# One attention-and-FFN block on one core: where the first FFN's residual x is saved, where its bias is added, and which engine widens and rounds

## What is computed

```
x = x + tanh(g_xattn[0]) * _L0_xattn_ref(ctx, ctx, _layernorm(x), ssm_kernel, D, 8)
x = x + tanh(g_ffn[0]) * _L0_ffn_ref(_layernorm(x), w1, b1, w2, b2)
x = x + tanh(g_xattn[1]) * _L1_xattn_ref(_layernorm(x), ctx, ...)
x = x + tanh(g_ffn[1]) * _L1_ffn_ref(_layernorm(x), ...)
```

```
def _dyn_quant_linear(x, w, b):
    qx, sx = _quant_per_tensor(x)      # one scale for all of x
    qw, sw = _quant_per_channel(w)     # one scale per output row of w
    acc = jnp.matmul(qx.astype(jnp.int32), qw.T.astype(jnp.int32))
    return acc.astype(jnp.float32) * (sx * sw) + b
h = _dyn_quant_linear(hidden_state, w1, b1)      # 512 -> 2048
h = jax.nn.gelu(h, approximate=False)
return _dyn_quant_linear(h, w2, b2)              # 2048 -> 512
```

## Time and profile before

| what | value |
|---|---|
| median of 3 runs | 641.4 us |
| the profiled execution, its own time | 643.1 us |
| its span (first to last instruction) | 641.3 us |
| PE, DVE, ACT, POOL busy | 95%, 85%, 74%, 55% |
| mean granted clock of PE | 0.997 |
| the 64 steps of `mm1` end, `mm2` starts | 283.4 us, 287.5 us |
| `mm2` ends on PE | 343.4 us |

### The profile page before, as it was taken

The page is one execution under the profiler, slowest core; times in us unless marked ns, Lnnn a source line. Parts: engine busy times, 40 slices in busy tenths (PEclk is TensorE's granted clock), DMA queues, the critical chain, the costliest instruction groups (busy, mean ns, idle before and its releaser), DMA issues.

```text
span 641.3 us, 9316 instructions
## 1 busy us (share of the span) xinstructions
PE 609.0 (95%) x2769; PEld 358.2 (56%) x2798; DVE 546.6 (85%) x1066; ACT 473.8 (74%) x718; POOL 351.9 (55%) x430
## 2 busy tenths in 40 slices
PE   5899999999999998989999999999888999999997
PEld 5777777777776443444445556555433444444443
DVE  2697888889999789976779988889898999999964
ACT  4469785765655896888672477766689999999984
POOL 1579888888874292310001111114487989898861
PEclk9999999999999999899999999999999999999999
DMA  8959896799999389838549920000116666656651
GB/s 300 377 192 310 291 327 223 260 323 339 332 299 331 134 285 311 223 94 327 198 98 167 255 56 16 16 17 17 50 33 162 185 177 183 164 180 164 182 162 50
DMA packets 141973, 125.20 MB, mean 195 GB/s; under 512 B 96032, under 2 KB 103984, under 8 KB 140784
## 3 DMA queue, kind: packets, MB, share of 16 engines
q1 hardware_dynamic: 134496, 110.52, 56.8%
q10 hardware_dynamic: 7440, 14.24, 6.6%
HBM read 68.04 MB, written 33.64 MB: 159 GB/s over the span
## 4 chain that ended last, share of the span: by engine, by line
PE 65%; DVE 12%; ACT 7%; issue 6%; DMA 4%; POOL 3%; SPq 2%; ACTq 0%; POOLq 0%; DVEq 0%
PE ps L1195 22%; PE ps L1475 14%; PE ps L1491 8%; PE ps L1313 4%; PE ps L1402 3%; PE ps L1432 3%; PE ps L1344 3%; DMA arena<-in_x 2%; ACT turn L989 2%; POOL arena L663 2%; PE ps L1450 2%; PE ps L1406 2%; SPq L446 2%; PE ps L1204 2%; DMA x_d<-arena 1%
## 5 line engine op out<-in xcount | busy, mean ns | idle before, releaser
L1195 PE MATMUL ps<-arena 128*128 128x288 f32 x640 | 160.6, 407 | 1.6 <-DVE inv_s L1661 0.9
L1195 PEld LDWEIGHTS ps<-arena 128*128 128x128 f32 x640 | 119.4, 190 | 33.5 <-DVE inv_s L1661 0.9
L1475 PE MATMUL ps<-arena 128*128 128x512 bf16 x510 | 113.5, 379 | 4.5 <-DVE arena L2066 4.3
L1475 PEld LDWEIGHTS ps<-arena 128*128 128x128 bf16 x512 | 49.4, 98 | 66.9 <-DVE arena L2066 5.7
L721 POOL TENSOR_TENSOR arena<-arena 128x512 f32<-128x512 f32 x64 | 80.4, 1276 | 8.6 <-DVE arena L2066 7.7
L618 POOL TENSOR_TENSOR arena<-arena 128x1024 f32<-128x1024 f32 x32 | 60.6, 1894 | 19.9 <-issue 12.3
L1313 PE MATMUL ps<-arena 128*128 128x512 bf16 (+1 forms) x249 | 57.1, 387 | 3.7 <-ACT arena L952 3.2
L1491 PE MATMUL ps<-arena 128*128 128x512 bf16 x241 | 57.1, 379 | 1.9 <-ACT arena L1103 0.7
L1344 PE MATMUL ps<-arena 128*128 128x512 bf16 x251 | 55.3, 379 | 1.2 <-DVE arena L1815 0.9
L952 ACT ACTIVATE arena<-ps,b,s 128x512 f32<-128x512 f32 x64 | 48.5, 778 | 10.6 <-DMA x_d<-arena 5.3
L625 POOL TENSOR_TENSOR turn<-turn 128x512 f32<-128x512 f32 x31 | 40.5, 1307 | 20.8 <-DVE turn L1638 20.8
(11 more groups left out here) (231 smaller groups left out, 1274.0 us busy)
## 6 DMA issues: line engine op xcount, KB each, us to landing
arena<-in_L_ffn_w SPq DMA_DIRECT2D x48, 512.0 KB, 6.2
arena<-kpad_d ACTq DMA_DIRECT2D x16, 512.0 KB, 7.1
hq_d<-arena SPq DMA_DIRECT2D x14, 512.0 KB, 2.6
tern_d<-late SPq DMA_DIRECT2D x24, 256.0 KB, 6.2
arena<-in_ctx SPq DMA_DIRECT2D x4, 1024.0 KB, 12.1
arena<-in_x SPq DMA_DIRECT2D x4, 1024.0 KB, 14.8
arena<-in_L_ffn_w ACTq DMA_DIRECT2D x8, 512.0 KB, 5.7
arena<-in_ctx SPq DMA_DIRECT2D x2, 2048.0 KB, 10.3
```

The source lines that it names most:

```text
L1195: last = pe.matmul(ps[:, 4 * s + lo, 0:NB * PAIRS], toep[:, u, (LB - 1 - lo + li) * P:(LB - lo + li) * P], kv[:, s, li, :], start=(li == 0 ...
L1475: last = pe.matmul(ps[:, bank, :], xq4T[:, s, 4 * j + k, :], w[:, k, c * L:(c + 1) * L], start=(k == 0), stop=(k == LB - 1))
```

## The change

1. SP saves x1 without its bias, as soon as each group of four tiles is complete: `x1_save(0)` and `(1)` follow the second `ctx_early` load, `(2)` and `(3)` the load of W2's block 0. They wait for the tiles (`x1_made`), no longer for POOL.
2. POOL adds the bias to `x_res` after it has come back, tile by tile in the order of use, after `partition_all_reduce`: 16 additions of 128 x 512 float32. DVE's `to_residual(k)` waits for `xb_added` of its tile in the place of `rows_in`.
3. `turned_widen(2)` and `(3)` move from DVE to POOL.
4. W2's blocks 2 and 3 are rounded by ACT, after 4 and after 12 gelus of the third group; DVE keeps blocks 0 and 1.
5. On SP, `w2_store(0)` moves ahead of the two transposing loads of x1.

```diff
+            def x1_save(g):
+                for n in range(G * g, G * g + G):
+                    x1_made(sp, n)
+                t = order1[G * g]
+                rows = slice(t, t + TB * (G - 1) + 1, TB)
+                sp.dma_start(x1_d[:, rows, :], x_res[:, rows, :]).then_inc(S["x1_saved"], 16)
+
+            x1_save(0)
+            x1_save(1)
             for c in range(4):
                 sp.wait_ge(tint_out[c], 16 * TC // 4)
             sp.dma_start(raw2[0], w2c[0]).then_inc(w2_in[0], 16)
+            x1_save(2)
+            x1_save(3)
...
-            x1_save(0)
             x1q_store(2)
             x1q_store(3)
-            x1_save(1)
+            w2_store(0)
             x1q_turned(2)
-            x1_save(2)
             x1q_turned(3)
-            w2_store(0)
-            x1_save(3)
             w2_store(1)
...
-            pool.wait_ge(S["b2_ready"], 1)
-            pool.wait_ge(S["xn1_ready"], NT)
-            pool.wait_ge(S["xqb_ready"], 3)
-            for t in order1[:10]:
-                pool.tensor_tensor(x_res[:, t, :], x_res[:, t, :], b2b[:, :], ALU.add).then_inc(S["xb_added"], 1)
-            pool.wait_ge(S["xqi_ready"], NG)
-            for t in order1[10:]:
-                pool.tensor_tensor(x_res[:, t, :], x_res[:, t, :], b2b[:, :], ALU.add).then_inc(S["xb_added"], 1)
+            def turned_widen(g):
+                rows = xqT[:, :, g * L:(g + 1) * L]
+                pool.wait_ge(w1_raw[g - 2], 16 * W1_LOADS + 16)
+                pool.tensor_scalar(rows, rows.bitcast(I16), 1.0, 0.0, ALU.mult, ALU.add).then_inc(S["xq_out"], 1)
+
+            turned_widen(2)
+            turned_widen(3)
...
+            pool.wait_ge(S["b2_ready"], 1)
+            for k in range(NT):
+                g = order2[k // G]
+                if k % G == 0:
+                    pool.wait_ge(rows_in[g], 32)
+                t = G * g + k % G
+                pool.tensor_tensor(x_res[:, t, :], x_res[:, t, :], b2b[:, :], ALU.add).then_inc(S["xb_added"], 1)
...
             act.wait_ge(S["x1_saved"], 16 * NG)
-            gelu(2, 0, range(FT))
+
+            def w2_quant(c):
+                act.wait_ge(S["w2_scaled"], c + 1)
+                act.wait_ge(tint_out[c - 2], 16 * TERN_STORES + 16)
+                act.activation(w2i[:, c % 2, :], raw2[c], ACT.Copy, scale=iw2[:, c:c + 1]).then_inc(S["w2_used"], 1)
+
+            gelu(2, 0, range(4))
+            w2_quant(2)
+            gelu(2, 0, range(4, 12))
+            w2_quant(3)
+            gelu(2, 0, range(12, FT))
...
-            turned_widen(2)
             for n in range(4):
                 hid_max(n + 4, 4 * L * n + 3 * FT * L)
-                if n == 0:
-                    turned_widen(3)
                 if n >= 2:
                     w2_scales(n)
-                    w2_quant(n)
...
             def to_residual(k):
                 t = G * order2[k // G] + k % G
-                if k % G == 0:
-                    v.wait_ge(rows_in[order2[k // G]], 32)
+                v.wait_ge(S["xb_added"], k + 1)
                 v.tensor_tensor(x_res[:, t, :], tmp2[:, k % 2, :], x_res[:, t, :], ALU.add).then_inc(S["x2_done"], 1)
```

More of the change, by code:

```diff
@@ L295, in x1_made @@
         def x1_made(eng, n):
-            if n in dve_adds:
+            if n < NT // 2:
+                eng.wait_ge(S["x1_dve"], 2 + n + 1)
+            elif n in dve_adds:
                 eng.wait_ge(S["x1_dve"], 2 + NT // 2 + dve_adds.index(n) + 1)
@@ L431, in _ @@
             sp.dma_start(raw2[1], w2c[1]).then_inc(w2_in[1], 16)
[L433 to L437, removed]
             def x1q_store(g):
@@ L1746, in rows_widen @@
                 v.tensor_copy(wqb[:, g % 2, :], wqi[:, g % 2, :]).then_inc(S["xqb_ready"], 1)
[L1749 to L1752, removed]
             hid_all = hid.rearrange("p q f n -> p (q f n)")
@@ L1767, in w2_quant @@
                 v.wait_ge(S["w2_scaled"], c + 1)
-                if c >= 2:
-                    v.wait_ge(tint_out[c - 2], 16 * TERN_STORES + 16)
                 v.tensor_scalar(w2i[:, c % 2, :], raw2[c], iw2[:, c:c + 1], None, ALU.mult).then_inc(S["w2_used"], 1)
```

## The result

| | before | after |
|---|---|---|
| median | 641.91 us (641.22 to 642.78, 4 runs) | 646.52 us (646.27 to 647.6, 4 runs) |
| profiled execution, its span | 643.1, 641.3 us | 646.3, 644.5 us |
| second product starts on PE | 287.53 | 282.76 |
| second product ends on PE | 343.44 | 347.74 |

The changed kernel is slower: its time is 1.0073 of before's, 95% interval 1.0054 to 1.0091. The forecast was 646.0, "slower" at 0.65. The span grew by 3.2 us. 4.8 us were won ahead of the second product, 9.1 lost in it, and 1.1 came back behind it. In its 55 executions beside the experiments the kernel before took 641.2 us in the median where its mean granted clock was 0.999 or 1.00 (14 of them) and 642.8 where it was 0.996 or 0.997 (38), and its profiled execution here (0.997) is of the second kind.

A forecast was written before the change was run, and what follows sets the result against it. PE, busy 609.0 of 641.3 us, was taken to bound the kernel. Front -4.4, rear +8.0 and attention +1.0 sum to +4.6, which on the median of 641.4 gives 646.0 us; range 637.0 to 649.5.

The forecast's parts named there:

- Front, -4.4: First FFN: with x1 saved early, PE's stop goes and the second product starts 4.4 us earlier; bounds 2.2 to 5.3.
- The other moved pieces cost nothing.: Front: POOL's widening of the turned rows, W2's block 3 rounding and what follows on SP and POOL cost 0.
- Who meets whom: Second product: DVE operations with two SBUF inputs and POOL's additions make each other wait; L1871, one SBUF input, does not.
- 1.9 us a tile: Second product: L1841 waits 0.63 and L1875 1.24 for POOL's additions, so DVE loses 1.9 us per tile.
- the alternating one: Second product: the port changes hands at each instruction's end, so POOL gets in twice a tile; PE's fourth group 10.0 late.
- "keep" of the widening at 446.7: Second product: DVE keeps the port if it asks again at once, so L1875 never waits behind L1841; stepping gives 6.0.
- The third group, 8.0 late: Second product: PE starts its third row group 8.0 us late, after a margin of 1.0, stepping with alternating turns.
- The fourth group, 2.0 more, and the clock "hidden": Second product: PE's fourth group starts 10.0 us late against the third's 8.0; a lower clock after the waits costs nothing.
- The rear's 8.0: Second product: additions meeting DVE cost 8.0 us, the middle of two ways of changing hands, 10.0 and 6.0.
- Attention, +1.0: Second attention, behind the second product: DVE, 1.6 us later than PE, delays its start; between none and all, 1.0.
- Only one-input operations wait: Rival, second product: L1841 and L1875 run undisturbed beside the additions; -4.4 + 0.7 = -3.7, 637.7 us; chance 0.23.
- The front did not fail: Rival, first FFN: ACT's roundings wait for scales or a W2 block, PE stops as before; +8.8, 650.2 us; chance 0.05.

The follow-up runs named there:

- e4: Kernel before, with only sixteen additions (bias plus bias into a free place, nothing waits for them) put on POOL in the rear: 647.59 us, ratio 1.0083.
- e10: Full changed kernel with parts 3 and 4 undone (widening and two roundings back on DVE), all sixteen additions kept: 646.5 us, ratio 1.0065.
- e7: Changed kernel without the sixteen additions, bias left out, and with the widening and two roundings back on DVE: 637.23 us, ratio 0.9929.
- e2: Changed kernel with its sixteen additions replaced by bias plus bias into a free place, DVE not waiting for them: 643.94 us, ratio 1.0013.
- e3: Changed kernel with twenty-four POOL memsets, which only write, in place of the additions; bias left out: 640.14 us, ratio 0.9969.
- e6: Changed kernel with eight bias sums in front and eight in the rear, each of these released by a DVE widening: 639.64 us, ratio 0.9966.
- e11: e9 with W2's block 0 stored behind the two transposing loads, as before the change (part 5 undone): 637.85 us, ratio 0.9932.
- e5: Changed kernel with the bias added in front again, three sums early, saves between the transposing loads, `w2_store(0)` behind them: 640.34 us, ratio 0.9976.
- e8: Changed kernel with only the first five of the sixteen additions, bias left out of the other eleven tiles: 640.44 us, ratio 0.9981.
- e9: e6 with parts 3 and 4 undone (widening and rounding of W2's blocks 2 and 3 back on DVE): 642.16 us, ratio 0.9995.

## Why the prediction was right, and where it was off

- **Front, -4.4.** Right: -4.77. The last gelu ended at 279.4 (279.2 said), DVE's scale for block 2 was there at 253.5 (253.6). Two things were off. PE's wait for the second rounding was 0.26, not 0.4. And the clock: 1.7 us of the gain is the 0.90 of the earlier trace rows, which the prediction named and did not price; it came in only because the step count was made at full clock. Against e4's front, which is before's with its clock kept, the gain is 285.37 - 282.76 = 2.6 us.
- **"The other moved pieces cost nothing."** Right in the changed kernel (e10). That they bring nothing was not said and holds too (e7, e10).
- **Who meets whom.** Right, and the step that carried the sign. DVE's two-input operations wait for POOL's additions (e2), not for the semaphore, and not for a POOL that only writes (e3). L1871's successor never waited.
- **1.9 us a tile.** Too high, 1.4. The order of turns was the alternating one: L1883 waited its 1.07 each time that it followed L1849 beside the additions, so the "keep" of the widening at 446.7 did not occur. The size failed: DVE's waits were 0.35 and 1.07, not 0.63 and 1.24. The prediction took the port to be held for an addition's whole 1.24 from start to start. POOL and DVE together needed 26.40 / 16 = 1.65 from one addition to the next; less DVE's 0.6 start to start, that leaves an estimate of 1.05 for the hold.
- **The third group, 8.0 late.** 6.1, by the same step: the first group lost 5.9 with its last widening, not 7.5. A small error the other way: 64 of 240 matmuls in 51.96 us are 13.86, not 13.7, so the slack was 0.7 and not 1.0. How the 8.0 and the 10.0 were stepped through, and the 276.4 of the front, the prediction doesn't show; their parts can't be compared one by one.
- **The fourth group, 2.0 more, and the clock "hidden".** The failed step. PE had no second stop. The clock fell instead and cost 2.9 us, more than the slack in which it was to hide. The alternating way, which is the one that occurred, had 10.0 for the whole; the runs have 6.1 + 2.9 = 9.0. The rear's 8.0 is close only because it was the middle with a way that did not occur, and because a clock priced at nothing made up for DVE's delay priced too high.
- **Attention, +1.0.** Wrong sign: -1.1 for all that lies behind the product. DVE's last sum of the product started 3.58 us later than before (352.00 against 348.42), PE's first matmul behind it 4.30: PE, slowed by its clock, was the later of the two, and DVE had caught up. PE's first wait for DVE in the attention ends 3.58 later too, in place of 4.30, so 0.7 of the 1.1 is this (before, then after):

```profile
355.12 1.96 PE L1406 MATMUL ps<-identf,arena 128*128 128x128 f32 x16 [1.08 <-DVE arena L1912]
```

```profile
358.70 1.97 PE L1427 MATMUL ps<-identf,arena 128*128 128x128 f32 x16 [0.36 <-DVE arena L1920]
```

  The other 0.4 came in the last FFN, which the change doesn't touch. Its cause is open, and e10, with the same additions, doesn't have it: its span is 644.9, 3.6 above before's.
- **Sum.** +4.6 said, +3.2 in span, +4.6 in the medians (646.52 - 641.91). The traces' difference is smaller because before's profiled execution was itself 1.2 us above its median and the changed kernel's 0.3 below. The forecast took its difference from the trace, whose front had a low clock, and put it on a median of 641.4, which lies with the executions that kept theirs. Its hit to half a microsecond is partly luck: 646.52 is 3.9 above the 642.64 that before took beside e10.
- **Rivals.** "Only one-input operations wait" is what e3 shows for writes, and falls for reads. The front did not fail, and the rear cost about twice what the front gave, not as much.

## What to carry to other kernels

Before work moves from a stage with slack on POOL to one where DVE paces PE, count the DVE instructions beside it that read two tensors in SBUF: each waited for the POOL instruction that reads SBUF, whatever its semaphores said. So did the one-input widenings; the sum of PSUM and SBUF (L1879) did not. If it must go there, start each piece by a signal that opens a known idle time of DVE (e6, e11); eight such additions cost 0.3 us in the second product, where sixteen in a row cost 9 and five in a row 2. And price a new stop of PE twice, once as a stop and once for the clock behind it; then look at the DMA issued just ahead of the one that the next stage waits for.

## What the runs showed that was not expected

- A POOL addition of two different tensors (1.27 us alone) held DVE up for some 1.07 us at most, one that reads one tensor twice for 0.83 (e2). The recorded duration of the POOL instruction overstates what it costs DVE.
- The clock's price jumped between small stops: 2.84, 2.41 and 1.35 us left it at 1.00 (e4's front, e5, e8), 3.23 took it to 0.90, and 3.27 in front of the second product of e9 made its first 16 matmuls 5.30 us long, where they take 3.61. Stops of 4.08 to 6.08 cost 1.7 to 2.9 us more, not in the order of their lengths.
